# Routing stage of a decoder layer: two DVE steps moved to the head of the round, three consumers moved by one or two rounds, the last eight lane factors made on DVE

## The reference

```python
x = x + attention(layernorm(x), Wq, Wk, Wv, Wo)     # 32 query heads, 8 key/value heads, rotary, causal
x = x + memory_read(layernorm(x), ctx, mask)        # softmax(h @ ctx.T / sqrt(512), masked) @ ctx, 64 context tokens
x = x + experts(layernorm(x), router, gate_up, down)
# experts: logits = h @ router.T + bias (8 experts); the two largest, softmax over the two;
#          each chosen expert: gate, up = h @ gate_up + bias; act = (clip(up) + 1) * gate * sigmoid(1.702 * gate);
#          y = act @ down + bias, weighted and summed
```

## Time and profile before

| What | Value |
|---|---|
| median of 3 runs | 1690.19 us |
| the profiled execution's own time | 1693.16 us |
| its span, first to last instruction | 1691.4 us |
| PE busy in the span | 1532.3 us, 91% |
| DVE busy | 1383.5 us, 82% |
| ACT busy | 1115.8 us, 66% |
| POOL busy | 1047.6 us, 62% |
| mean granted TensorE clock | 0.938 of full |

### The profile page before, as it was taken

How to read it: one execution, slowest core, us unless ns; L and a number is a source line. 1 busy time by engine, 2 the same in 40 slices (tenths; PEclk the granted TensorE clock), 3 DMA queues, 4 the chain that set the end, 5 groups by cost and what they waited for, 6 DMA issues and landing times. The chain is left out here.

```text
span 1691.4 us, 31714 instructions
## 1 busy us (share of the span) xinstructions
PE 1532.3 (91%) x8951; PEld 1324.5 (78%) x8951; DVE 1383.5 (82%) x3470; ACT 1115.8 (66%) x2593; POOL 1047.6 (62%) x1161
## 2 busy tenths in 40 slices
PE   5799999999999999999999998699499999999994
PEld 4687877887787787887777877498388888888883
DVE  7898888898898898898898887477588888888882
ACT  3788878778777877787777877322165555555651
POOL 6589779789679779779769866546522233222321
PEclk9999999999999999999999999755599999999997
DMA  4000000000000000000000000112468778877765
GB/s 169 1 14 20 1 14 20 1 13 19 1 13 19 1 13 19 1 13 19 1 13 0 1 1 1 40 69 88 166 177 226 219 208 215 230 220 208 191 169 131
DMA packets 62002, 124.47 MB, mean 74 GB/s; under 512 B 20942, under 2 KB 21070, under 8 KB 61792
## 3 DMA queue, kind: packets, MB, share of 16 engines
q1 hardware_dynamic: 51408, 102.24, 18.8%
q0 software_dynamic: 10304, 20.59, 6.7%
q10 hardware_dynamic: 144, 0.07, 0.0%
HBM read 106.08 MB, written 24.71 MB: 77 GB/s over the span
## 5 line engine op out<-in xcount | busy, mean ns | idle before, releaser
L522 POOL TENSOR_SCALAR probs<-probs,row_inv 128x512 f32<-128x512 f32 (+3 forms) x512 | 280.6, 567 | 25.6 <-DVE row_inv L426 25.6
L306 ACT ACTIVATE probs<-probs,neg_max 128x512 f32<-128x512 f32 (+3 forms) x512 | 281.5, 552 | 10.5 <-DVE neg_max L419 6.8
L419 DVE CUSTOM_DVE_ANT_0 probs<-bank,causal 128x512 f32<-128x512 f32 (+3 forms) x512 | 220.6, 485 | 57.3 <-PE bank L208 43.8
L1209 POOL DMA_INDIRECT acc<-ctx_raw,idx x46 | 74.5, 1619 | 311.0 <-ACT ctx_raw L1362 300.5
L218 PE MATMUL bank<-ident,probs 128*128 128x128 f32 x1280 | 187.4, 277 | 53.6 <-POOL probs L522 35.7
L407 DVE TENSOR_TENSOR pt_lo<-bank,pt_hi 128x512 fp32r<-128x512 f32 (+1 forms) x384 | 214.9, 586 | 22.8 <-ACT pt_hi L299 22.7
L218 PEld LDWEIGHTS bank<-ident,probs 128*128 128x128 f32 x1280 | 150.3, 142 | 101.0 <-issue 45.7
L513 POOL TENSOR_TENSOR rot<-rot,sin 128x512 f32<-128x512 f32 (+1 forms) x96 | 123.9, 1291 | 166.0 <-DVE rot L438 162.5
L1290 PE MATMUL bank<-xt_hi,gu_hi 128*128 128x256 f32 x736 | 208.0, 283 | 1.5 <-DVE xt_lo L407 1.5
L1290 PE MATMUL bank<-xt_hi,gu_lo 128*128 128x256 f32 x736 | 206.4, 280 | 0.0
L1290 PE MATMUL bank<-xt_lo,gu_hi 128*128 128x256 f32 x736 | 206.2, 280 | 0.0
(11 more groups left out here) (204 smaller groups left out, 4209.2 us busy)
## 6 DMA issues: line engine op xcount, KB each, us to landing
gu_raw<-in_gate_up SPq DMA_DIRECT2D x92, 512.0 KB, 3.7
dn_raw<-in_down SPq DMA_DIRECT2D x92, 256.0 KB, 3.6
w_raw<-in_wqkv SPq DMA_DIRECT2D x8, 768.0 KB, 4.5
w_raw<-in_wo_rows SPq DMA_DIRECT2D x8, 512.0 KB, 3.5
h_rows<-ln_h SPq DMA_DIRECT2D x16, 256.0 KB, 2.0
acc<-x_res SPq DMA_DIRECT2D x4, 1024.0 KB, 4.6
x_res<-in_x SPq DMA_DIRECT2D x3, 1024.0 KB, 11.2
ctx_raw<-in_ctx SPq DMA_DIRECT2D x2, 512.0 KB, 6.8
```

The costliest lines, as they stand in the source:

```text
L306: nc.scalar.activation(row, row, ACT.Exp, bias=neg_max[:, hb, i:i + 1], scale=-1.0, accum_out=row_sum[:, hb, i:i + 1]).then_inc(s["exp_don ...
L419: nc.vector.tensor_tensor_reduce(out=probs[:, hb, P_AT[i]:P_AT[i] + (i + 1) * P], in0=S_BANK[k][:, at:at + (i + 1) * P], in1=causal[:, (QB ...
L522: nc.gpsimd.tensor_scalar(row, row, row_inv[:, hb, i:i + 1], 0.0, ALU.mult, ALU.add).then_inc(s["pnorm_done"], 1)
```

## The change

Three edits. DVE makes dve_at and dve_ht at the head of its round instead of behind the statistics. The constants become 2, 3, 4, 5, 7, 8 instead of 1 to 6: everything from the transpose of ln_t on comes one round later, and from the transpose of ln_h on two rounds later (there are 27 rounds instead of 25). The eight at_lane instructions of the last quarter are made by DVE behind its at_row instead of by POOL.

```diff
@@ dve_q_rows
             nc.vector.tensor_tensor(at_row[:, :, :], lane_iota[:, :].unsqueeze(1).to_broadcast([P, 2 * QB, P]),
                                     pos_f[:, 0, :].unsqueeze(2).to_broadcast([P, 2 * QB, P]), ALU.is_equal).then_inc(z["row_done"], 1)
+            if q == B - 1:
+                for n in range(2 * QB):
+                    t = q * QB + n // 2
+                    nc.vector.tensor_scalar(at_lane[:, n, :], lane_iota[:, :], pos_f[:, 1, n:n + 1], tok_id[:, t:t + 1],
+                                            ALU.is_equal, ALU.mult).then_inc(z["lane_done"], 1)
@@ constants
-        M_AT, EXP_AT, READ_AT, ADD_AT, H_AT, TOP_AT = range(1, 7)
+        M_AT, EXP_AT, READ_AT, ADD_AT, H_AT, TOP_AT = 2, 3, 4, 5, 7, 8
         ROUNDS = TT + TOP_AT + 3
@@ DVE's list
+                    on(lambda t: dve_at(dve, t), k, READ_AT)
+                    on(lambda t: dve_ht(dve, t), k, H_AT)
                     on(lambda t: dve_logits(dve, t), k, TOP_AT)
                     on(lambda t: dve_m_scores(dve, t), k, EXP_AT)
                     on(lambda t: dve_logits_sum(dve, t), k, TOP_AT)
...
-                    on(lambda t: dve_at(dve, t), k, READ_AT)
-                    on(lambda t: dve_ht(dve, t), k, H_AT)
                     on(lambda t: dve_m_sum(dve, t), k, EXP_AT)
@@ POOL's list
-                    on_q(lambda q: pool_q_lanes(pool, q), k, 2)
+                    on_q(lambda q: pool_q_lanes(pool, q) if q < B - 1 else None, k, 2)
```

## The result

The kernel after takes 1714.42 us (median of 4 runs, 1712.49 to 1716.19) against 1690.31 us (median of 4 runs, 1689.7 to 1697.43) for the kernel before: a ratio of 1.0134, 95% interval 1.0119 to 1.0149, or +24.1 us. Predicted were 1715.7 us and +25.5.

A forecast was written before the change was run, and what follows sets the result against it. PE was taken to bound the routing stage, whose changes reach the end one to one. Terms 19.4 + 0 + 6.4 - 0.3 + 0 = +25.5 us on a median of 1690.2 gave 1715.7 us, range 1708 to 1721.

The forecast's parts named there:

- What bounds the stage: Routing stage: PE bounds the rounds, taking its list in order; it waits only 2.3 us in eleven rounds of before.
- The wait that was computed: Routing rounds: PE's memory scores wait for DVE's masked scores, behind h_lo of the same round; 1.97 us a round.
- The rounds: Eleven rounds with scores and ln_h transposes: 6.24 to 8.21 us each, 21.7 us less 2.3 of old waits, +19.4 us.
- The first rounds: Start of the routing stage: three rounds of 5.4 us, no net change, 0, between -1 and +1 us.
- The drain: End of the routing stage, after round 17: one ln_h round more to run, +6.4 us, bounds +3 and +9.
- The last lane factors: Place step to index product, last quarter: eight lane factors on DVE, 9.7 us for 9.98; -0.3 us, from -1.0 to +1.1.
- The gather and the weights: Start of the expert stage: later first weights have room, as PE's experts wait on the gather; 0, within 2 us.
- The wait is hidden: Rival, routing rounds: masked scores reach PE in time, rounds stay at 6.24 us; 1692 us, no change; chance 0.05.
- DVE falls behind: Rival, rounds with place and at_row: DVE too is late, another 3 to 8 us, 1719 to 1724 us; chance 0.12.
- The clock rises: Rival, routing stage: TensorE stays at the higher clock level, rounds of some 5.8 us, total about 1686 us; chance 0.04.
- the transposes, which the prediction sets apart: TensorE's clock in the routing stage: transposes do not engage the full clock as other products do; argued against a rise.

The follow-up runs named there:

- Experiment 4: Two kernels: before with only the constants 2, 3, 4, 5, 7, 8, 1688.68 us; before with only the last quarter's eight lane factors on DVE, 1690.2 us.
- Experiment 1: Before with only dve_at and dve_ht moved to the head of DVE's round, constants 1 to 6 kept: 1726.54 us, ratio 1.0206.
- the first of 5: After with dve_at and dve_ht behind the x_res addition, ahead of indices and statistics, and constants 2 to 7: 1700.5 us, ratio 1.0054.
- kernel of experiment 5 with both extra rounds: After with only dve_at and dve_ht moved behind the x_res addition, constants 2, 3, 4, 5, 7, 8 kept: 1684.06 us, ratio 0.9955, the fastest kernel.
- the masked scores first: After with only DVE's masked scores put ahead of dve_at and dve_ht: 1703.38 us, ratio 1.0068.
- experiments 1 to 3: Before with dve_at and dve_ht at the head, 1726.54 us; after with masked scores ahead of them, 1703.38; after with only dve_at at the head, 1701.66.
- the lane factors alone: Before with only the last quarter's eight lane factors made by DVE: 1690.2 us, ratio 0.9997.
- experiment 5: After with dve_at and dve_ht behind the x_res addition: constants 2 to 7, 1700.5 us; these with ln_h's norm first, 1688.41; after's constants, 1684.06.
- the shared version (5 and 3): After with dve_at and dve_ht mid-round, constants 2 to 7, ln_h's norm first; last quarter's lane factors five on POOL, three on DVE: 1689.16 us.

## Why the prediction was right

**What bounds the stage.** PE in order, as predicted: what stops PE costs. The wait that was computed came at the place, in the eleven rounds and with the releaser named (18.8 us there, near 20 forecast). The three in the first rounds are part of the rounds of 5.4 us that the prediction gave them; they took 5.3.

**The rounds, +19.4 predicted, +14.8 in the profiled executions.** Rounds 7 to 17 took 88.4 us (the sum above) against 73.6 for rounds 6 to 16 of before (1105.44 to 1179.01). That is just outside the term's own bounds, 15 to 22. The wait in a round was sized well: the delay of the scores was 1.93 us for 1.97, from h_lo to the masked scores 0.68 for 0.72, from there to PE 0.37 for 0.38, the round 8.15 for 8.21. What made the term too large in this execution is mainly the two rounds in the higher clock, 3.3 us; 14.8 + 3.3 = 18.1. The runs' median stands 1.9 us above this execution. I did not see the reason for its clock.

**The first rounds, 0 predicted, -1.5.** Tile 5's round starts at 1103.67 on PE instead of 1105.21; the bound was -1.

**The drain, +6.4 predicted, +7.1.** From the end of the last round with scores to the lane factors of quarter 2:

```profile
1196.19 0.77 PE L880 MATMUL bank<-ctx_hi,a_st 128*128 128x512 f32 x1 [2.66 <-DVE x_res L1156]
1204.40 0.76 PE L880 MATMUL bank<-ctx_hi,a_st 128*128 128x512 f32 x1 [2.64 <-DVE x_res L1156]
1209.84 0.99 PE L899 MATMUL bank<-rw_t,h_hi 128*128 128x16 f32 x4 [1.78 <-DVE logits L999]
...
1216.77 7.35 POOL L1101 TENSOR_SCALAR at_lane<-lane_iota,pos_f,tok_id 128x128 fp32r<-128x128 f32 x8 [3.13 <-DVE pos_f L1084]
```

It ran from 1192.26 to 1216.77, 24.5 us against the 23.8 computed and 17.4 before. With no scores left to cover it, the read waits for the x_res addition as the text said. Experiment 4 bounds the depth's own share of it: with the low parts in their old place the extra rounds raised PE's idle time by 4.5 us in all.

**The last lane factors, -0.3 predicted, -1.05.** From place to index product 8.93 us (1225.18 to 1234.11) for 9.98. Two sizes were off. The eight took 2.05 us together (1227.62 to 1229.67), 0.26 each, where I had taken 0.31 from a smaller form. And from the copy of counts to the index product it took 4.44 us (1229.67 to 1234.11), where I had taken 4.74 from before, in which POOL worked beside it. The Trainium skill (VectorE: DVE Perf Modes, section Mode 2x_2P), with two float32 elements a cycle, gave an estimate 0.5 us below mine for the eight. The trace gives 0.43 below, so it agrees in size, though one form can't show the mode.

**The gather and the weights, 0 predicted.** 10.15 for 10.6 us.

The terms as measured: -1.5 + 14.8 + 7.1 - 1.05 = +19.35, with the index product at +19.3.

**What is luck in it.** The forecast of +25.5 is 6.2 us above what the same terms came to in the two traces. That the medians differ by 24.1, only 1.4 less than forecast, is owed to which executions were profiled: before's took 2.9 us more than its median, after's 1.9 less, together 4.8 us that no trace shows term by term. The mechanism and the size of one wait were right; the closeness of the total is in part luck.

**The rivals.** *The wait is hidden* fell with the first timeline. *DVE falls behind* fell too, though DVE had nothing to spare: in the round that starts at 1150.90 it came to the last instruction, behind at_row, at 1160.71, 9.8 us later where 10.0 was computed. The next low part of a_st started 1.94 us into its round instead of 1.93, and no wait for the masked scores exceeds 1.7 us. (The stretch of 9.91 us above is not DVE's doing: it holds PE's eight slot products, which rounds of before have too.) *The clock rises* was right in one point and wrong in its consequence: the clock did rise in the stage, in two rounds of eleven, and each such round got shorter (6.08 and 6.81 us). But it did not stay there, and a price of 0.04 for a gain stands. My reason against it was weak, however: I held that added idle time speaks against a rise, and the stage's mean in before (0.51) and after (0.52) is about the same with 21 us more of it.

**What the reasoning lacked** shows in the expectations of experiments 1, 4 and 5 rather than in the prediction: none has a price for the clock, though two of them name it. Experiment 1 came out 14 us above its expected value, with 5.8 us of busy time more than before; experiment 4 came out 5 us below, with 12.5 less; the first of 5 came out 7 us above, with 13.3 more than experiment 4.

## What to carry to other kernels

Before a step moves to the head of an engine's list, take each bank with a single reader and ask whether that reader now stands behind something that the waiting engine must itself produce in the same round; if so, the two engines wait for each other once per round, however idle both look. Put low-part copies behind the readers that free banks (here the masked scores and the x_res addition), and give their consumers the extra round only as far as the norm behind them needs it. In a stage where the clock is granted only at times, compare PE's busy and idle time over the same products separately, or a change of clock is taken for an effect of the edit.

## What the runs showed of the hardware that I had not expected

**TensorE's clock in a busy stage.** The same 521 products took between 99.46 and 119.30 us of PE's time, with mean granted clocks of the stage from 0.61 to 0.50. In before, one plain round follows the other without a gap, and the clock stays at 0.50, the lower level, through nearly all of it. In the kernel of experiment 5 with both extra rounds, whole rounds ran at the higher level:

```profile
1109.88 0.66 PE L855 MATMUL bank<-ident,ln_t 128*128 128x128 f32 x4
...
1111.23 1.10 PE L865 MATMUL bank<-ctx_t,xt 128*128 128x64 f32 x8
1112.16 0.47 PE L880 MATMUL bank<-ctx_hi,a_st 128*128 128x512 f32 x1
...
1113.76 0.66 PE L855 MATMUL bank<-ident,ln_t 128*128 128x128 f32 x4
```

This round took 3.9 us; its transposes 0.66 instead of 1.11, its scores 1.10 instead of the 1.81 of a gapless round of before. Over all kernels the stage's means can be put into two groups, though they touch. The five that have the new or nearly new constants and no stall in every round had 0.57 to 0.61; all others had 0.50 to 0.56 (0.56 with the masked scores first). Of those, after and experiments 1 to 3 and the first of 5 stall once a round; before and the lane factors alone (0.51 both) have no such stall, but the old constants. Neither condition was varied with all else kept, and each mean is of one profiled execution.

One execution is not enough for it. The 23 runs of the kernel before that stand beside the first kernels of experiment 5 go from 1686.09 to 1695.24 us, and the mean clock of their whole span goes with it: 0.943 to 0.944 in the three fastest, 0.934 to 0.937 in the four slowest. The profiled execution of before (1693.16 us, 0.938) is one of the slower, so its 0.51 in the stage need not be what this kernel mostly gets. For the fastest kernel there is more: its five runs lie within 1.4 us of one another at 0.942 to 0.944, and the runs of before beside it that had 0.942 or 0.943 took 1689.04 to 1691.56 us. So its gain is not just a run with a high clock. But what decides the clock of the stage was not isolated, and how much of it the order of the steps earns stays open. The Trainium skill (TensorE: Matmul & The Clock Gate, Part 1) has sustained activity end the throttling; taken by itself that does not agree with the gapless rounds at 0.50. Whether the transposes, which the prediction sets apart, account for it no run here shows; once the higher level was granted they ran at it.

**POOL's first lane factor beside DVE.** In the shared version (5 and 3) POOL's first of its lane factors took 1.9 us, and its five 5.34 us in all. That does not come from the sharing: before's first of the last eight took 1.82 us too, the others 0.79 to 0.98. In both kernels it started 0.06 us behind DVE's at_row, which takes 1.2 us. Where POOL came to it after at_row had ended, the first took 0.81 and the eight 6.23 us, as for quarter 0 in after (DVE, then POOL):

```profile
1159.57 1.22 DVE L1087 TENSOR_TENSOR at_row<-lane_iota,pos_f 128x1024 fp32r<-128x1024 f32 x1
...
1161.42 6.23 POOL L1101 TENSOR_SCALAR at_lane<-lane_iota,pos_f,tok_id 128x128 fp32r<-128x128 f32 x8
```

So about 1 us of POOL's time goes when it starts beside this DVE instruction. Four on POOL and four on DVE gave 0.5 us of trace time against eight on DVE, and nothing in the runs.
